# Quantised cross attention with a gated LoRA step on one core: a new program order, and the second batch's context coded on GpSimd

## The reference

```
def _L0_xattn_ref(x1, x2, x1_scale, x1_zp, x2_scale, x2_zp):
    ...
        q = jnp.clip(jnp.round(x / s + z), QMIN, QMAX)      # 0 to 255
        return (q - z) * s
    ...
    return jnp.matmul(q1, q2)
def _L0_ffn_ref(x, A, B, Wr):        # A (4, 16, 2048), B (4, 2048, 16), Wr (4, 2048)
    logits = flat @ Wr.T
    topk_vals, topk_idx = jax.lax.top_k(logits, TOP_K)      # 2 of 4
    ...
    gates = jax.nn.softmax(sparse, axis=-1)
    mid = jnp.einsum('tf,erf->ter', flat, A)
    all_deltas = jnp.einsum('ter,eor->teo', mid, B) * SCALE
    delta = jnp.sum(gates[:, :, None] * all_deltas, axis=1)
...
x = x + jnp.tanh(g_xattn[0]) * _L0_xattn_ref(_layernorm(x, axis=-1), ctx_4096, ...)
x = x + jnp.tanh(g_ffn[0]) * _L0_ffn_ref(_layernorm(x, axis=-1), L0_ffn_A, L0_ffn_B, L0_ffn_Wr)
```

## Time and profile before

| | |
|---|---|
| median of 3 runs | 423.1 us (422.08 to 425.37) |
| profiled execution | 423.39 us, its span 421.7 us |
| busy: PE, DVE, ACT, POOL | 355.9, 314.9, 260.8, 85.6 us |
| moved by DMA | 68.51 MB, mean 162 GB/s |
| mean granted TensorE clock | 0.958 of 2.4 GHz |

### The profile page before, as it was taken

How to read it: one execution, slowest core, us unless ns; L and a number is a source line. 1 busy time by engine, 2 the same in 40 slices (tenths; PEclk the granted TensorE clock), 3 DMA queues, 4 the chain that set the end, 5 groups by cost and what they waited for, 6 DMA issues and landing times. The chain is left out here.

```text
span 421.7 us, 7130 instructions
## 1 busy us (share of the span) xinstructions
PE 355.9 (84%) x2352; PEld 207.1 (49%) x2352; DVE 314.9 (75%) x732; ACT 260.8 (62%) x240; POOL 85.6 (20%) x74
## 2 busy tenths in 40 slices
PE   0075569489898999989898999999999999999974
PEld 0032324265545454645555565656565656565552
DVE  2469994889877878787878777777777777676684
ACT  1757796578868585868777465656555565656150
POOL 1000000222222040403122222222313231314030
PEclk9999759779999999999999999999999999999986
DMA  4999980269474645465552322222322222312022
GB/s 143 331 400 426 427 371 2 99 209 307 185 234 133 210 145 189 181 184 173 195 203 101 100 103 101 99 99 99 99 99 99 99 99 99 102 50 101 0 101 100
DMA packets 22240, 68.51 MB, mean 162 GB/s; under 512 B 3204, under 2 KB 3716, under 8 KB 20100
## 3 DMA queue, kind: packets, MB, share of 16 engines
q1 hardware_dynamic: 22216, 68.20, 45.3%
HBM read 51.42 MB, written 16.78 MB: 162 GB/s over the span
## 5 line engine op out<-in xcount | busy, mean ns | idle before, releaser
L538 PE MATMUL ps_main<-q,q1T 128*128 128x512 f16 x928 | 212.1, 379 | 0.0
L538 PEld LDWEIGHTS ps_main<-q,q1T 128*128 128x128 f16 x928 | 87.7, 98 | 101.0 <-issue 7.0
L404 ACT ACTIVATE h_hi<-x,small_tile 128x1024 f16<-128x1024 f32 x32 | 39.4, 1233 | 61.6 <-DVE small_tile L825 61.6
L350 POOL TENSOR_TENSOR h_lo<-work,h_hi 128x1024 f16<-128x1024 f32 x31 | 66.7, 2151 | 46.1 <-ACT work L408 44.3
L809 DVE SCALAR_TENSOR_TENSOR x<-ps_main,small_tile,xt 128x512 f32<-128x512 f32 x60 | 44.7, 746 | 24.2 <-DMA out_x<-x 14.8
L787 DVE BATCH_NORM_STATS2 small_tile<-xt 128x6 f32<-128x512 f32 x64 | 40.7, 682 | 19.8 <-DMA xt<-in_x 19.8
L344 POOL TENSOR_TENSOR small_tile<-small_tile 128x1 f32<-128x1 f32 x16 | 8.8, 551 | 200.8 <-DVE small_tile L821 200.8
L390 ACT ACTIVATE x_byte<-xt,small_tile 128x1024 uint8<-128x1024 f32 x32 | 38.1, 1233 | 16.2 <-DVE small_tile L803 16.2
L814 DVE BATCH_NORM_STATS2 small_tile<-x 128x6 f32<-128x512 f32 x64 | 44.3, 692 | 1.7
L883 DVE TENSOR_TENSOR x<-ps_delta,x 128x512 f32<-128x512 f32 x64 | 42.3, 683 | 2.7 <-PE ps_delta L604 2.7
L383 ACT ACTIVATE ctx_stage<-ctx_stage,small_tile 128x1024 uint8<-128x1024 f32 x32 | 38.7, 1233 | 3.4 <-DMA ctx_stage<-in_ctx 3.4
(11 more groups left out here) (97 smaller groups left out, 367.8 us busy)
## 6 DMA issues: line engine op xcount, KB each, us to landing
xt<-in_x SPq DMA_DIRECT2D x32, 512.0 KB, 3.8
q<-in_ctx SPq DMA_DIRECT2D x16, 1024.0 KB, 18.0
ctx_stage<-in_ctx SPq DMA_DIRECT2D x32, 512.0 KB, 5.4
out_x<-x SPq DMA_DIRECT2D x64, 256.0 KB, 2.2
x<-in_L_ffn_A SPq DMA_DIRECT2D x1, 512.0 KB
x<-in_L_ffn_B SPq DMA_DIRECT2D x1, 512.0 KB, 14.9
small_tile<-in_L_xattn_x_scale SPq DMA_DIRECT2D x2, 0.5 KB, 4.0
small_tile<-in_L_xattn_x_zp SPq DMA_DIRECT2D x2, 0.5 KB, 4.3
```

Of the source, the lines that this page charges most:

```text
L350: nc.gpsimd.tensor_tensor(h_lo[:, h, :], work[:, h, :], h_hi[:, h, :], ALU.subtract).then_inc(h_lo_ready, 1)
L404: nc.scalar.activation(h_hi[:, h, :], x1[:, b % 2, half(h)], ACT.Identity, bias=h_bias[:, :], scale=h_rstd[:, :]).then_inc(h_hi_ready, 1)
L538: mm = pe.matmul(acc[:, :], q1T[:, b % 2, k, :], q2[:, batch(b), k, cols(n)], start=(k == 0), stop=(k == KT - 1))
```

## The change

Nearly every function is rewritten; tiles and steps keep their meaning.

- x and the sum share a ring of four tiles, `xr`, in place of `xt` and `x1`.
- The three scales and points and two gates come in one load of six numbers. A and the router come transposed as columns, B transposed and twice, so PE turns neither. A is divided by a power of two for each column and kept in two f16 parts (`largest_of_a`, `powers_of_a`, `copy_scales` on DVE, `split_a` on GpSimd); B is multiplied by the gain and split on DVE (`high_of_b`, `low_of_b`). A is staged in `xr[3]`, B in `ctx_stage[1]`.
- During loading PE takes tile 0 and, from row 4 on, three banks of tile 1.
- All of a tile's q1 is scaled, turned (into ps_gate) and copied at once; tiles 0 and 1 are copied by DVE.
- The second batch's rows come whole through two stages; GpSimd, not DVE, turns their bytes into codes (`code_ctx`), three for each of the tiles 4 to 7.
- PE puts gates and LoRA between parts of main; delta of tile b - 2 is done in slot b.

Lines not marked are as in the kernel before; the common indentation is cut.

```
-a_parts = sb("a_parts", [P, KT, 3, J], BF16)
+a_parts = sb("a_parts", [P, KT, 2, J], F16)
...
+first_banks = [ps_main + ps_delta, [ps_mid] + ps_turn + [ps_main[0]],
+           [ps_main[1], ps_delta[0], ps_delta[1], ps_main[0]]]
...
+def load_ctx(k):
+    wait(sp, ctx_coded, k - STAGES + 1)
+    if k == 1:
+        sp.wait_ge(b_ready, 1)
+    sp.dma_start(ctx_stage[:, k % STAGES, :], ctx_pairs[(KT + k) // 2, k % 2, :, :]).then_inc(ctx_loaded[k % STAGES], 16)
...
+load_x(0)
+load_row(0)
+load_row(1)
+load_x(1)
+for k in range(2, 12):
+    load_row(k)
+load_x(2)
+for k in range(12, KT):
+    load_row(k)
+sp.dma_start(a_raw, lora_a).then_inc(a_loaded, 16)
+sp.dma_start(b_raw, lora_b).then_inc(b_loaded, 16)
+load_ctx(0)
+sp.wait_ge(a_ready, 1)
+load_x(3)
+load_ctx(1)
+load_ctx(2)
+c = 3
...
+    else:
+        store(b - 2, range(2), HALF)
+        if b + 2 < TILES:
+            load_x(b + 2)
+        todo = 3
+    for _ in range(todo):
+        if c < KT:
+            load_ctx(c)
+            c += 1
...
+def split_a():
+    a_view = a_raw.rearrange("p (k j) -> p k j", j=J)
+    pool.wait_ge(a_loaded, 16)
+    pool.wait_ge(a_scale_ready, 1)
+    nc.gpsimd.tensor_tensor(a_view, a_view, scales[:, 1, :].unsqueeze(1).to_broadcast([P, KT, J]), ALU.mult).then_inc(a_part_step, 1)
+    pool.wait_ge(a_part_step, 1)
+    nc.gpsimd.tensor_copy(a_parts[:, :, 0, :], a_view).then_inc(a_part_step, 1)
+    pool.wait_ge(a_part_step, 2)
+    nc.gpsimd.tensor_tensor(a_parts[:, :, 1, :], a_view, a_parts[:, :, 0, :], ALU.subtract).then_inc(a_ready, 1)
+def code_ctx(k):
+    pool.wait_ge(ctx_scaled, k + 1)
+    nc.gpsimd.tensor_scalar(q2[:, 1, k, :], ctx_byte[:, k % STAGES, :], neg_centre[:, 1:2], None, ALU.add).then_inc(ctx_coded, 1)
+power_x(0)
+power_x(1)
+power_x(2)
+split_a()
+power_h(0)
+low_part(0, 0)
+power_h(1)
+low_part(0, 1)
+code_ctx(0)
+power_x(3)
+low_part(1, 0)
+low_part(1, 1)
+code_ctx(1)
+power_h(2)
+low_part(2, 0)
+low_part(2, 1)
+code_ctx(2)
+power_x(4)
+code_ctx(3)
+c = 4
+for b in range(4, TILES):
+    power_h(b - 1)
+    low_part(b - 1, 0)
+    low_part(b - 1, 1)
+    if b < LAST:
+        power_x(b + 1)
+    for _ in range(3):
+        if c < KT:
+            code_ctx(c)
+            c += 1
+power_h(LAST)
...
+scale_x(0)
+scale_row(0)
+scale_row(1)
+scale_row(2)
+scale_x(1)
+for k in range(3, 13):
     scale_row(k)
+scale_x(2)
+scale_row(13)
+scale_row(14)
+scale_row(15)
+copy_q1T(2)
+scale_ctx(0)
+high_part(0)
+normal_half(0, 0)
+normal_half(0, 1)
+copy_hiT(0, 0)
+copy_hiT(0, 1)
+scale_ctx(1)
+copy_loT(0)
+gate_exp(0)
+scale_x(3)
+high_part(1)
+normal_half(1, 0)
+normal_half(1, 1)
+copy_q1T(3)
+copy_hiT(1, 0)
+copy_hiT(1, 1)
+scale_ctx(2)
+copy_loT(1)
+high_part(2)
+normal_half(2, 0)
+normal_half(2, 1)
+gate_exp(1)
+copy_hiT(2, 0)
+copy_hiT(2, 1)
+scale_ctx(3)
+copy_loT(2)
+scale_x(4)
+gate_exp(2)
+copy_q1T(4)
+c = 4
+for b in range(4, TILES):
+    high_part(b - 1)
+    normal_half(b - 1, 0)
+    normal_half(b - 1, 1)
+    if c < KT:
+        scale_ctx(c)
+        c += 1
+    copy_hiT(b - 1, 0)
+    copy_hiT(b - 1, 1)
+    if b < LAST:
+        scale_x(b + 1)
+    copy_loT(b - 1)
+    if b < LAST:
+        copy_q1T(b + 1)
+    if c < KT:
+        scale_ctx(c)
+        c += 1
+    gate_exp(b - 1)
+    if c < KT:
+        scale_ctx(c)
+        c += 1
+high_part(LAST)
+copy_hiT(LAST, 0)
+copy_hiT(LAST, 1)
+copy_loT(LAST)
+gate_exp(LAST)
...
+def mid_lo(b, h):
+        mm = pe.matmul(ps_mid[:, J:2 * J], hT[:, h, k, :], a_parts[:, kk, 0, :], start=False, stop=(kk == KT - 1))
...
+    for k in range(KT):
+        if k == JOIN - 1:
+            turn_q1(1, 0)
+        if k == KT - 2:
+            turn_q1(2, 0)
+        pe.wait_ge(row_coded, k + 1)
+        for n in range(NB):
+            product(0, n, k, general)
+        if k == JOIN:
+            pe.wait_ge(q1T_ready, 2)
+            for kk in range(k):
+                for n in range(3):
+                    product(1, n, kk, general)
+        if k >= JOIN:
+            for n in range(3):
+                product(1, n, k, general)
+    main(1, 3, general)
+    scales_of_a()
+    main(2, 0, general, 0, 8)
+    spread_scales()
+    main(2, 0, general, 8)
+    main(2, 1, general)
+    turn_hi(0)
+    main(2, 2, general, 0, 10)
+    high_and_turn_low(0)
+    main(2, 2, general, 10)
+    low(0)
+    main(2, 3, general, 0, 14)
+    turn_gate(0, 3)
+    main(2, 3, general, 14)
+    turn_q1(3, 1)
+    turn_hi(1)
+    main(3, 0, general, 0, 4)
+    delta(0, 0)
+    main(3, 0, general, 4)
+    delta(0, 2)
+    high_and_turn_low(1)
+    main(3, 1, general, 0, 8)
+    low(1)
+    main(3, 1, general, 8)
+    turn_hi(2)
+    main(3, 2, general, 0, 10)
+    turn_gate(1, 4)
+    high_and_turn_low(2)
+    main(3, 2, general, 10)
+    low(2)
+    main(3, 3, general, 0, 8)
+    delta(1, 0)
+    main(3, 3, general, 8, 14)
+    turn_gate(2, 4)
+    main(3, 3, general, 14)
+    delta(1, 2)
+    turn_q1(4, 3)
...
+            main(b, 0, general, 0, 4)
+            delta(b - 2, 0)
+            main(b, 0, general, 4)
+            delta(b - 2, 2)
+            main(b, 1, general)
+        turn_hi(b - 1)
+        main(b, 2, general, 0, 10)
+        high_and_turn_low(b - 1)
+        main(b, 2, general, 10)
+        if b < LAST:
+            turn_q1(b + 1, b - 1)
+        low(b - 1)
+        main(b, 3, general, 0, 14)
+        turn_gate(b - 1, min(b + 2, TILES))
+        main(b, 3, general, 14)
+    delta(LAST - 1, 0)
+    delta(LAST - 1, 2)
+    turn_hi(LAST)
+    high_and_turn_low(LAST)
+    low(LAST)
+    turn_gate(LAST, TILES)
+    last_delta()
...
+def copy_q1T(b):
+    dve.wait_ge(q1_turned, b + 1)
+    nc.vector.tensor_scalar(q1T[:, b % 2, :, :].rearrange("p (j two) m -> p j two m", two=2),
+                            as16(ps_gate, U8).rearrange("p (j m two) -> p j two m", m=P, two=2),
+                            neg_centre[:, 0:1], None, ALU.add).then_inc(q1T_ready, 1)
...
+def high_of_b():
+    dve.wait_ge(b_loaded, 16)
+    nc.vector.tensor_scalar(lora_bT[:, :], b_raw, gain[:, 1:2], None, ALU.mult).then_inc(b_step, 1)
+def low_of_b():
+    dve.wait_ge(b_step, 1)
+    nc.vector.scalar_tensor_tensor(out=lora_bT[ER:P, :], in0=b_raw[ER:P, :], scalar=gain[ER:P, 1:2],
+                                   in1=lora_bT[ER:P, :].bitcast(F32), op0=ALU.mult, op1=ALU.subtract).then_inc(b_ready, 1)
...
+stats_x(0, 0)
+stats_x(0, 1)
+var_x(0)
+rests_of_points()
+scale_of_x(0)
+copy_q1T(0)
+code_row(0)
+stats_x(1, 0)
+stats_x(1, 1)
+var_x(1)
+code_row(1)
+scale_of_x(1)
+code_row(2)
+copy_q1T(1)
+for k in range(3, 12):
+    code_row(k)
+stats_x(2, 0)
+stats_x(2, 1)
+var_x(2)
+code_row(12)
+scale_of_x(2)
+for k in range(13, KT):
+    code_row(k)
+largest_of_a()
+add_main(0, 0)
+add_main(0, 1)
+add_main(0, 2)
+add_main(0, 3)
+stats_h(0, 0)
+stats_h(0, 1)
+powers_of_a()
+stats_h(0, 2)
+stats_h(0, 3)
+var_h(0, steps_h(0))
+copy_scales()
+add_main(1, 0)
+add_main(1, 1)
+bias_h(0)
+add_main(1, 2)
+add_main(1, 3)
+for n in range(NB):
+    stats_h(1, n)
+var_h(1, steps_h(1))
+high_of_b()
+add_main(2, 0)
+bias_h(1)
+low_of_b()
+add_main(2, 1)
+stats_h(2, 0)
+copy_loT(0)
+stats_h(2, 1)
+add_main(2, 2)
+rank_gates(0)
+stats_h(2, 2)
+weigh(0)
+stats_x(3, 0)
+stats_x(3, 1)
+var_x(3)
+split_gate(0)
+scale_of_x(3)
+add_main(2, 3)
+stats_h(2, 3)
+var_h(2, steps_h(2))
...
+        split_gate(b - 2)
+        add_main(b - 1, 3)
+        stats_h(b - 1, 3)
+        var_h(b - 1, steps_h(b - 1))
+        add_delta(b - 2, 0)
+        bias_h(b - 1)
+        add_delta(b - 2, 1)
+        if b < LAST:
+            stats_x(b + 1, 0)
+        add_main(b, 0)
+        stats_h(b, 0)
+        add_delta(b - 2, 2)
+        add_delta(b - 2, 3)
+        if b < LAST:
+            stats_x(b + 1, 1)
+            var_x(b + 1)
+        add_main(b, 1)
+        stats_h(b, 1)
+        if b < LAST:
+            scale_of_x(b + 1)
+    copy_loT(b - 1)
+    add_main(b, 2)
+    rank_gates(b - 1)
+    stats_h(b, 2)
+    weigh(b - 1)
+split_gate(LAST - 1)
+add_main(LAST, 3)
...
+for h in range(2):
+    nc.vector.tensor_tensor(h_lo[:, half(h)], work[:, h, :], h_hi[:, half(h)], ALU.subtract).then_inc(h_lo_ready, 1)
+for n in range(1, NB):
+    add_delta(LAST - 1, n)
+copy_loT(LAST)
+rank_gates(LAST)
+weigh(LAST)
+split_gate(LAST)
```

More of the change, by code:

```diff
@@ L516, in rests @@
                 r2 = [rest_part[:, c, 1:2].to_broadcast([P, BANK]) for c in range(3)]
-                for k in range(KT):
+                with pe.Fori(0, KT) as k:
                     for c in range(3):
@@ L596, in delta, with high_and_turn_low, low, turn_gate @@
-            def delta(b, i, first):
-                wait(pe, gT_step, b, i, 1, 1)
+            def high_and_turn_low(b):
+                for h in range(2):
+                    mid_hi(b, h)
+                    turn_lo(b, h)
+            def low(b):
+                for h in range(2):
+                    mid_lo(b, h)
+            def turn_gate(b, q1):
+                pe.wait_ge(gated_ready, b + 1)
+                pe.wait_ge(q1T_ready, q1)
```

(19 more changed lines are left out.)

985 lines of the change are left out of this document (365 added, 620 removed).

## The result

The changed kernel takes 470.3 us (median of 4 runs, 469.8 to 470.8) against 423.7 in the same series: ratio 1.110, interval 1.105 to 1.115. The forecast was 412.4, range 401 to 427. The profiled execution has a span of 468.8.

What follows compares the result with a forecast made beforehand. PE was taken to bound slots 8 to 15, waits and DVE's coding to slow the first batch. main(4, 0) at 141, plus 88 and 2.5, then 158.4 less 0.4 gave 389.5; tail 21.2 made 410.7, reported 412.4, range 401 to 427.

Steps and rivals of the forecast that it cites:

- Step 4: Slots 4 to 7: coding moves from DVE to GpSimd, slots take 22.0 against 22.8, main(8, 0) at 231.5.
- c = 1.9: Slots 4 to 7: time in us of one row code on GpSimd, three a slot, making its slot 11.1 of 22.
- rival A: Slots 4 to 7: GpSimd pays the two-input rate, c = 4.3, slots of 25, total 420 to 428; chance 0.14.
- Rival B: First batch: GpSimd bounds it from c = 5.5 on, 450 with c = 8; chance 0.09 with other losses over 428.
- c = 8: Slots 4 to 7: Rival B's example price of a GpSimd code, twice L350, giving a GpSimd slot of 29.4 and 450.
- the slot of 22.0: Slots 4 to 7: load landed 18.4, scale_ctx to 20.5, gate_exp 20.7, weigh 0.9, turn_gate 0.2, two matmuls 0.43.
- Step 2: Tiles 0 to 3: waits use up the start's lead; main(3, 0) near 110, main(4, 0) at 141 against 142.33.
- Step 1: Loading: earlier row loads, row 15 coded at 59.6, tile 0 and three banks of tile 1 done near 62.
- Steps 3 and 5: Fewer columns of A make PE's tile 19.8 for 20.68; slots 8 to 15 take 8 x 19.8 = 158.4.
- Step 6: Tail: changes around the last tile shorten it from 22.7 by 1.5 to 21.2.
- the saved wait (-1.7): Tail: four banks let the second pair of delta go without waiting for add_delta, saving 1.7.

Runs made afterwards that it cites:

- e12: Changed kernel, row codes back on VectorE, lists of loads, exponents, head and tail reordered, main(8, 0) waiting for the last row only before its last block: 414.0 us, ratio 0.979.
- e13: e12 with the sixteen second-batch row codes on GpSimd again (tensor_scalar, 5.44 us each), power_h ahead of each slot's third code: 431.5 us, ratio 1.019.
- e4: Changed kernel with a series of GpSimd and VectorE operations on unused buffers behind its end, to price them; only those rows are read, the whole time means nothing.
- e5: Changed kernel with GpSimd's code as a tensor_copy (1.89 us) in place of tensor_scalar, leaving out the zero point's subtraction: 447.9 us, ratio 1.058.
- e3: Changed kernel, GpSimd coding, with gate_exp(b - 1) ahead of the second scale_ctx on ScalarE: 472.9 us, ratio 1.113.
- e11: Changed kernel with each GpSimd code replaced by three memsets of the same row, as long but without coding: 465.0 us, ratio 1.095.
- e1: Changed kernel with the second batch's sixteen row codes back on VectorE: 447.0 us, ratio 1.056.
- e10: Changed kernel, VectorE coding, first row load first, head reordered, exponent ahead of second scale_ctx (also slots 2 and 3), add_delta(14, 1) ahead of tile 15's work halves: 430.6 us.
- e14: e13 with the GpSimd code as a tensor_copy of 1.89 us, leaving out the zero point's subtraction: 409.4 us, ratio 0.967.
- e2: Kernel before with only its half-row codes (32) moved from VectorE to GpSimd: 425.2 us, ratio 1.003.
- e6: e1 with the first row load of each slot ahead of store(b - 2) and load_x(b + 2) from b = 5 on: 446.2 us, ratio 1.054.

## Why the prediction failed, by its steps

**Step 4, the price of a code, c = 1.9: measured 5.44.** The sum took the rate of `affine_select` because the operation has one input, and set the two-input row (4.3) as the upper bound. The truth lay above that bound, so rival A (4.3) was not far enough either, though its chain (power_h and bias_h behind the codes) is one of the two that came. Rival B, GpSimd as the bound from c = 5.5 on, is nearly what came: its busy time is 21.6 a slot, more than e12's whole slot, though even in e13 it is not busy all the time (21.6 of 25.7). The time lies above B's 450 as well. B had 9% because "no row comes near 4 ns an element", but that was the argument against c = 8; the point from which B decides is 2.7 ns. The Trainium skill (GPSIMD Engine Reference, Engine selection), with its "1-input is roughly line-rate", speaks for the error; e4 has that rate for a copy (1.89) and not for `tensor_scalar` (5.44), and the measurement decides. Worth: e5 against the changed kernel, 22.4 us.

**Step 4, the slot of 22.0.** Even at c = 1.9 it was 27 (e5). The chain was named rightly (store, x, row load, scale_ctx, gate_exp, weigh), but two terms were too small. The load was taken as issued at 12.5 and landed at 18.4 in the slot. In e5's slot 6, the one of 29.0, it was issued at 13.1 and landed at 21.2 (main(6, 0) at 205.2), and in the changed kernel at 13.8 and 21.9 (main(6, 0) at 219.3). And nothing was put in for VectorE waiting beside GpSimd: in e5 3.2 us between the exponent and the gates (L857 1.73 for 0.21, L865 2.06 for 0.35), in the changed kernel 3.4 of L857's 3.58. The 2.8 and the 3.2 make the forecast's 22.0 into 28.0. What such a wait costs does not simply add up, as e3 and e11 show: behind each stood another of equal length (power_h behind the codes). What the step missed is that the slot is a cycle, in which every late item delays its own successor: a buffer freed late, a load late, an exponent late, a bias late.

**Step 2, tiles 0 to 3: main(4, 0) forecast at 141, measured at 161.6.** The waits before turn_hi(0) (4.5 for 5), low(0) (8.1 for 7) and turn_q1(3) (4.8 for 6) were right; main(3, 0) came at 118.0 for 110, because the start ended 5 later and the two steps on B took 6.2 for 3.5 (`low_of_b` 3.84 for 2.2, beside a low part), so that the load behind `b_ready` went out at 93.4 for 85.4. Slot 3 was forecast at 31 and took 43.6. Its waits are 14.3 in sum for the 5 put in: gates of tiles 1 and 2 waited 6.1 and 3.5 for 1, partly beside GpSimd's codes. PE's work is 29.3 for 25.8, with the clock granted at 0.81 where the sum had 1.5 us for it. e1 puts GpSimd's share at about 7 (154.9 for 161.6); the rest is order, and e12 has main(4, 0) at 142.5.

**Step 1, start.** Row 15 was coded at 65.0 for 59.6. Parameters landed at 7.1 for 5, and the first `turn_q1` began at 19.1, 3.9 behind the bytes that it turns (15.2), where the sum has it right behind them. PE's sequencer was in a branch on the flag of the zero points' remainders (L707) for 6.1 us, from 12.9 to 19.0; in the kernel before the same branch (L697) takes 6.0. The sum has no term for it. ScalarE's idle 4 us before scale_x(2) came as forecast (4.63).

**Steps 3 and 5** were right: sixteen matmuls of 68 columns take 0.50, half the price, so 0.46 a tile is saved where 0.25 was put in, and slots are 19.7 for 19.8.

**Step 6, the tail: 21.2 forecast, 25.4 measured.** From turn_gate(15) to the end it takes 7.5 for 8.9, so most of the saved wait (-1.7) is there, but the second half of delta(14, 2) waited 4.95 for add_delta(14, 1) (0.3 before), queued on VectorE behind both h_lo subtractions; it was not in the list of what stands behind what. e10 took most of it away.

In short, of 58 us 22 are the price. The other 36 lie, by e5's trace, before main(3, 0) (8), in slot 3 (6), in slots 4 to 7 (16) and in the tail (4): about 5 are the start, most of the rest are orders that the sum treated as fitting. The forecast time itself is that of a program with lists mended and c = 1.9: e14, at 409.4. Open stays why `tensor_scalar` is so much dearer than a copy on GpSimd, and which trait of the old program makes it bear the long code (e2) where the mended new one does not (e13).

## What to carry to other kernels

Price an operation on GpSimd by a row of the same operation, not by one with as many inputs; where there is none, the upper bound is open, and the case in which that engine's sum passes the slot deserves weight. In lists written out by hand, write for every step what stands ahead of it on its engine and when that is ready: an exponent behind a row that waits for a DMA, or a power behind a code, costs more than either operation. Mend such a cycle as a whole: single reorderings (e3, e6) gave nothing, and together with the engine put right they gave 56 us.

## What was not expected of the hardware

- GpSimd's `tensor_scalar` took 5.44 us for 2048 elements of bytes, f16 or float32 alike, against 1.89 for its copy, 1.80 for memset and 4.04 for a two-input f16 sum.
- Beside it a VectorE operation from SBUF to SBUF took up to 5.32 us for 0.25 (64 elements, one input), one with a PSUM input or statistics no longer than usual, and memset held up nothing. A two-input product was let go 1.7 before the code's end. In turn a VectorE row code made GpSimd's 1.03 longer.
- The granted clock was 0.81 in slot 3, with waits of 6.1 and 3.5 us, and 0.88 in slots 4 to 7, with waits of 4.8 to 7.3 in each. It was 1.00 in e12's slots 5 to 7, where PE's longest wait is 1.7; of e13's two slots above, with waits of 1.9 in each, one is at 0.93 and one at 1.00. The six matmuls behind a long wait took 2.77, 1.3 us more than the 1.46 that they take in e10 without one.
- A branch in PE's own program took 6.1 us (6.0 in the kernel before), and no matmul began before it was through.
